# A four-layer graph network on one core: one-hot products of 250 columns in fp32 (728 steps) in place of 500 columns in three bf16 parts (572 steps), and a gathered-row add moved from TensorE to VectorE

## The reference, cut to what matters

```python
h = relu(layernorm(x)); e = edge_attr_16 @ We + be
aggr = segment_sum(relu(h[src] + e), dst)              # layer 0
x = x + gelu((h + aggr) @ W1 + b1) @ W2 + b2
...
wn = w * inv_sqrt_out[src] * inv_sqrt_in[dst]          # layer 1, ten steps
h = 0.9 * segment_sum(h[src] * wn, dst) + 0.1 * h0
...                                                    # layer 2: three attention layers over the edges; layer 3: edge convolution
```

## Time and profile before

| | |
|---|---|
| median of 3 runs | 4460.14 us (4458.2 to 4472.35) |
| span of the profiled execution | 4458.5 us |
| its own time | not listed apart; nothing is known to lie around the span |
| first pass (first to last one-hot and ReLU on VectorE) | about 654 to 1363 us |
| busy over the span | TensorE 71%, VectorE 62%, GpSimd 67%, ScalarE 21% |

### The profile page before, as it was taken

The page is one execution under the profiler, slowest core; times in us unless marked ns, Lnnn a source line. Parts: engine busy times, 40 slices in busy tenths (PEclk is TensorE's granted clock), DMA queues, the critical chain, the costliest instruction groups (busy, mean ns, idle before and its releaser), DMA issues.

```text
span 4458.5 us, 80594 instructions
## 1 busy us (share of the span) xinstructions
PE 3158.4 (71%) x19947; PEld 2109.2 (47%) x19958; DVE 2785.2 (62%) x10030; ACT 933.1 (21%) x3282; POOL 2993.2 (67%) x3059
## 2 busy tenths in 40 slices
PE   1240118888887999999678885888758788566665
PEld 1240004454443444343466664666646666445554
DVE  6970229998894111111688887888878888765554
ACT  0000003443341000000122222222212222112121
POOL 2677767777667888850377774777747777467776
PEclk9999999999997999999899997999979999755555
DMA  4310013333348999999322223222232222211112
GB/s 142 110 45 10 17 63 85 86 87 87 80 88 278 364 355 361 357 358 359 109 63 62 62 62 52 63 62 63 61 51 62 62 62 61 34 32 28 28 28 30
DMA packets 295308, 497.96 MB, mean 112 GB/s; under 512 B 165612, under 2 KB 210541, under 8 KB 293675
## 3 DMA queue, kind: packets, MB, share of 16 engines
q1 hardware_dynamic: 120119, 340.02, 21.7%
q0 software_dynamic: 92160, 115.39, 14.1%
q10 hardware_dynamic: 82800, 40.01, 3.1%
HBM read 435.66 MB, written 59.08 MB: 111 GB/s over the span
## 4 chain that ended last, share of the span: by engine, by line
PE 28%; POOL 25%; issue 19%; DMA 13%; DVE 10%; DVEq 1%; ACT 1%; SPq 1%; POOLq 0%; another core or an unknown queue 0%; ACTq 0%
PE ps L1545 26%; POOL arena L814 18%; DMA arena<-table,arena 10%; POOL rows_dst L797 7%; DMA rows_dst<-stage,arena 1%; DVE arena L1150 1%; DVE arena L1132 1%; PE ps L1730 1%; DMA arena<-in_edge_attr_dram 1%; DVE arena L1149 1%; DVEq L542 1%; DVE arena L1134 1%; DVE arena L1168 1%; DVE arena L1164 1%; DVE arena L1319 0%
## 5 line engine op out<-in xcount | busy, mean ns | idle before, releaser
L814 POOL DMA_INDIRECT arena<-table,arena x2080 | 2091.1, 1005 | 1104.3 <-issue 562.9
L1545 PE MATMUL ps<-arena 128*128 128x96 f32 (+3 forms) x9176 | 1473.3, 337 | 599.7 <-DVE arena L1168 252.4
L1545 PEld LDWEIGHTS ps<-arena 128*128 128x128 f32 (+3 forms) x9176 | 1025.4, 196 | 1017.5 <-issue 641.9
L1545 PE MATMUL ps<-arena,nodes 125*64 125x500 f32 (+2 forms) x3144 | 651.1, 538 | 33.4 <-DMA arena<-dense 22.8
L1150 DVE TENSOR_SCALAR arena<-iota_row_b,arena 128x128 f32<-128x128 bf16 x2080 | 579.9, 297 | 0.0
L768 POOL DMA_INDIRECT rows_src<-stage,stage_at x400 | 477.3, 1193 | 117.1 <-issue 109.3
L797 POOL DMA_INDIRECT rows_dst<-stage,arena x400 | 395.4, 989 | 223.3 <-issue 123.2
L1162 DVE TENSOR_TENSOR arena<-ps,arena 128x256 f32<-128x256 f32 x416 | 176.3, 424 | 531.6 <-DMA arena<-table,arena 516.4
L1149 DVE TENSOR_SCALAR arena<-iota_row_b,arena 128x128 bf16<-128x128 bf16 x1664 | 456.0, 276 | 2.1 <-DVE arena L1302 0.7
L1545 PEld LDWEIGHTS ps<-arena,nodes 125*64 125x64 f32 (+1 forms) x3144 | 242.6, 137 | 353.5 <-issue 321.1
L1251 DVE TENSOR_TENSOR nodes<-nodes,ps 125x256 f32 (+1 forms) x70 | 27.5, 392 | 608.4 <-PE ps L1730 608.4
(11 more groups left out here) (285 smaller groups left out, 3605.4 us busy)
## 6 DMA issues: line engine op xcount, KB each, us to landing
arena<-dense SPq DMA_DIRECT2D x240, 750.0 KB
nodes<-dense SPq DMA_DIRECT2D x60, 750.0 KB
dense<-arena ACTq DMA_DIRECT2D x150, 250.0 KB
arena<-table,arena POOLq DMA_INDIRECT x2080
arena<-dense SPq DMA_DIRECT2D x60, 500.0 KB, 7.7
arena<-rows_dst SPq DMA_DIRECT2D x208, 96.0 KB
arena<-dense SPq DMA_DIRECT2D x6, 2000.0 KB, 21.8
arena<-pair_rows SPq DMA_DIRECT2D x12, 976.6 KB
```

Source lines behind the costliest of these rows:

```text
L814: nc.gpsimd.indirect_dma_start(rows[:, u, k, 0:width], None, frm, bass.IndirectOffsetOnAxis(ap=p[:, c, j, c_other:c_other + 1].bitcast(I32 ...
L1545: return nc.tensor.matmul(to, lhsT, rhs, start=start, stop=stop, skip_group_check=True)
```

## The change

A bin is split for the steps: a step now covers two source blocks (250 columns), so that a destination block has 13 step groups, in place of 7. Eviction still goes by the bins of 4 blocks. A step is one fp32 product (no split of the weight). There are `T - 1 + SBINS - HI` = 715 real steps, padded to 728, 56 per body, 7 in every turn. The tables grow from 576 to 728 entries, and their bank and bin columns are now summed up from per-bin differences (`gone_bank`, `gone_need`). The identity product of the gathered rows goes away; VectorE adds `rows` to the edge term with a tensor_tensor and then makes the ReLU in a second instruction behind a semaphore.

```diff
-PER2 = 11
-PER_U = (5, 6)
+SB, SBG = 2, 13
+SBW = SB * LO
+SBINS = HI * SBG
+SCH = -(-SBINS // LO)
+PER2 = 14
+PER_U = (7, 7)
-TABLE_W = 576
+TABLE_W = STEPS_D
...
-        lhs = carve([128, PER2, 3, 128], BF16)
-        rhs = carve([128, PER2, CW], BF16)
+        lhs = carve([128, PER2, 128])
+        rhs = carve([128, PER2, SBW])
...
-            for g in range(CG):
-                nc.vector.tensor_scalar(rel_key[:, g, :], src_blk, float(-g * CW), None, ALU.add)
-            for part in range(3):
-                link(nc.vector.tensor_copy(w_parts[:, :, part], w_left[:, part, :]))
-                if part < 2:
-                    link(nc.vector.tensor_tensor(w_left[:, part + 1, :], w_left[:, part, :], w_parts[:, :, part], ALU.subtract))
+            for g in range(SBG):
+                ins = nc.vector.tensor_scalar(rel_key[:, g, :], src_blk, float(-g * SBW), None, ALU.add)
+            link(ins)
...
-                    if (first + k) % 2:
-                        nc.vector.scalar_tensor_tensor(
-                            lhs[:, slot], iota_row_b[:].unsqueeze(1).to_broadcast([128, 3, 128]), lo_col[:, bass.ds(tile_at, 1)],
-                            w_parts[:, bass.ds(tile_at, 1), :].rearrange("p o c -> p (o c)").unsqueeze(2).to_broadcast([128, 3, 128]),
-                            ALU.is_equal, ALU.mult)
-                    else:
-                        for part in range(3):
-                            nc.vector.tensor_scalar(lhs[:, slot, part, :], iota_row_b[:], lo_col[:, bass.ds(tile_at, 1)],
-                                                    w_left[:, part, bass.ds(tile_at, 1)], ALU.is_equal, ALU.mult)
-                    nc.vector.tensor_scalar(rhs[:, slot, :], iota_col_h[:], flat_keys[:, bass.ds(key_at, 1)], None,
+                    nc.vector.tensor_scalar(lhs[:, slot, :], iota_row_b[:], lo_col[:, bass.ds(tile_at, 1)],
+                                            w_col[:, bass.ds(tile_at, 1)], ALU.is_equal, ALU.mult)
+                    nc.vector.tensor_scalar(rhs[:, slot, :], iota_col_h[:, 0:SBW], flat_keys[:, bass.ds(key_at, 1)], None,
                                             ALU.is_equal).then_inc(op_ready, 1)
...
                 v.wait_ge(lin_ready, i * U + (u + 1))
-                nc.vector.tensor_scalar(of(msg, u)[:, :, 0:D], lin(u), 0.0, None, ALU.max).then_inc(msg_ready, 1)
+                v.wait_ge(gathered[u], 16 * K * (i + 1))
+                nc.vector.tensor_tensor(of(s1, u)[:, 0], lin(u), rows[:, u, :, 0:D], ALU.add).then_inc(sum_ready, 1)
+                v.wait_ge(sum_ready, i * U + (u + 1))
+                nc.vector.tensor_scalar(of(msg, u)[:, :, 0:D], of(s1, u)[:, 0], 0.0, None, ALU.max).then_inc(msg_ready, 1)
...
-                    for part in range(3):
-                        ins = mm(flat[:, bass.ds(step_at["bank", first + k], CW)], lhs[:, slot, part, :], rhs[:, slot, :], start=False, stop=False)
-                    ins.then_inc(built, 1)
+                    mm(flat[:, bass.ds(step_at["bank", first + k], SBW)], lhs[:, slot, :], rhs[:, slot, :],
+                       start=False, stop=False).then_inc(built, 1)
...
-                mm(ps[:, 4 + u % 2, 0:K * D], of(payT, u), wl0[:].rearrange("p k d -> p (k d)"))
-                pe.wait_ge(gathered[u], 16 * K * (i + 1))
-                mm(lin(u), ident[:], rows[:, u, :, 0:D], start=False).then_inc(lin_ready, 1)
+                mm(ps[:, 4 + u % 2, 0:K * D], of(payT, u), wl0[:].rearrange("p k d -> p (k d)")).then_inc(lin_ready, 1)
```

More of the change, by code:

```diff
@@ L59 @@
 BINS = HI * CG
-PER2 = 11
-PER_U = (5, 6)
+SB, SBG = 2, 13
+SBW = SB * LO
+SBINS = HI * SBG
+SCH = -(-SBINS // LO)
+SBIN_CHUNKS = [(h, min(LO, SBINS - h * LO)) for h in range(SCH)]
+assert SBG == -(-HI // SB) and CB == 2 * SB and CG == -(-SBG // 2)
+PER2 = 14
+PER_U = (7, 7)
 PER_BODY = PER2 * U // 2
 STEPS_D = NB * PER_BODY
-TABLE_W = 576
-assert STEPS_D >= T - 1 + BINS - HI and STEPS_D <= TABLE_W and HI - (CG - 1) * CB == 1
+TABLE_W = STEPS_D
+assert STEPS_D >= T - 1 + SBINS - HI and TABLE_W <= 2 * 512 and HI - (CG - 1) * CB == 1
 EV = 2
@@ L233, in gnn_kernel @@
         iota_t = carve([128, TABLE_W])
[L234 removed]
+        bin_col = carve([128, 5 * SCH])
+        gone = carve([128, 2, SCH])
+        gone_d = carve([128, 2, SCH])
+        gone_g = carve([128, 2, SCH])
+        gone_pair = carve([128, 2, SCH])
+        gone_turn = carve([128, 2, SCH])
+        gone_need = carve([128, SCH])
+        gone_bank = carve([128, SCH])
         start_col = carve([128, 2])
[L236 removed]
+        bin_end_f = carve([1, SBINS])
         tables_from = used[0]
[L239 removed]
+        begun = carve([128, SCH, TABLE_W])
         bin_of = carve([1, TABLE_W])
@@ L1063, in _, with down_by @@
-            for h, n in enumerate((LO, BINS - LO)):
+            def down_by(to, frm, n):
+                link(nc.vector.tensor_scalar(to, frm, 1.0 / n, -(0.5 - 0.5 / n), ALU.mult, ALU.add))
+                link(nc.vector.tensor_scalar(to, to, ROUND, None, ALU.add))
+                link(nc.vector.tensor_scalar(to, to, -ROUND, None, ALU.add))
+            for x in range(2):
+                for h in range(SCH):
+                    ins = nc.vector.tensor_scalar(gone[:, x, h:h + 1], iota_p[:], float(h * LO - x), None, ALU.add)
@@ new lines, in _ @@
+            link(ins)
+            down_by(gone_d, gone, SBG)
+            link(nc.vector.scalar_tensor_tensor(gone_g, gone_d, -float(SBG), gone, ALU.mult, ALU.add))
+            down_by(gone_pair, gone_g, 2)
+            link(nc.vector.scalar_tensor_tensor(gone_g, gone_pair, -2.0, gone_g, ALU.mult, ALU.add))
+            link(nc.vector.scalar_tensor_tensor(gone_d, gone_d, float(CG), gone_pair, ALU.mult, ALU.add))
+            down_by(gone_turn, gone_d, EV)
+            link(nc.vector.scalar_tensor_tensor(gone_turn, gone_turn, -float(EV), gone_d, ALU.mult, ALU.add))
@@ L1064, in _ @@
+            for h, n in SBIN_CHUNKS:
                 ins = nc.vector.tensor_scalar(begun[0:n, h, :], iota_t[0:n, :], bin_col[0:n, h:h + 1], None, ALU.is_ge)
```

81 lines of the change are left out of this document (40 added, 41 removed).

## The result

| | before | after |
|---|---|---|
| median of the runs side by side | 4464.36 us (4 runs, 4458.2 to 4472.35) | 4497.35 us (4 runs, 4495.15 to 4504.7) |
| ratio, 95% interval | | 1.0077 [1.0062, 1.0093] |
| span of the profiled execution | 4458.5 us | 4495.1 us |
| first to last step of the first pass | 657.4 to 1362.3, 704.9 us | 659.8 to 1399.0, 739.2 us |

The changed kernel is 33 us slower; the forecast was 17 to 18 us. The difference is 0.8%, small but clear of its interval. The first and last step are those of the register operation that stands ahead of each dense step in TensorE's queue. I read the pass by them from here on, since they can be counted in every kernel; the forecast's 709 us for the pass before runs from VectorE's first instruction to its last, 4.1 us more.

A forecast was written before the change was run, and what follows sets the result against it. TensorE's queue was to replace VectorE as the first pass's bound: 676 + 33 + 18 = 727 us, 18 over 709. With 1.5 us less before the pass, span 4475 us, forecast 4477 us; range 4422 to 4518 us.

The forecast's parts named there:

- The queue becomes the bound: First pass: TensorE's queue keeps 0.467 us a step, needs 676 us, above VectorE's 648 us.
- rival 1: First pass: VectorE stays the bound as the queue's interval falls to 0.40 us; 36 us less, 4423 us; chance 0.20.
- The gaps of 2.8 and 4.0 us: TensorE's queue between turns: 2.8 us with one group of register loads, 4.0 with two; six long, two short a body.
- The waits on the queue: TensorE in the first pass: 33 us for banks, 3 to fill, 5 for jumps, 10 where VectorE is later.
- The bank term: TensorE's queue waits for the eviction to empty one of two banks: 33 us of the first pass.
- Now it is hidden behind VectorE.: Kernel before, first pass: TensorE's queue needs 557 us, 150 us under the 709 that VectorE sets.
- VectorE's work: VectorE in the first pass: seven steps of 0.51 us, add and longer ReLU 0.37 us more; 5.4 us a turn.
- The refills at the loop's jump: VectorE's queue refilling at a body's start: 5.5 us instead of 3.6, twelve times.
- The prologue, 1.5 us less: Preparation before the first pass: three casts and two linked subtractions go, six keys come; 1.5 us less.
- The clock: TensorE's granted clock in the first pass is kept, 0.96 before; under 0.9 would show the forecast wrong.
- rival 3: TensorE's clock falls: 4686 us at 1.2 GHz throughout, 4503 us for a tenth of the turns; chance 0.08.
- GpSimd: GpSimd's gathers in the first pass take 5.9 us a turn, under TensorE's 6.5: hidden.

The follow-up runs named there:

- a shorter eviction: Changed kernel without the clearing of a bank after its eviction (ScalarE's second copy): 4474.17 us, ratio 1.0046 to the kernel before.
- short queue: No increment behind the bank wait, bank and need in one table, one register load per four steps: changed kernel 4424.7 us, kernel before 4424.9 us.
- the half products: Changed kernel with dense products of 125 columns instead of 250: 4510.19 us (1.0111); also without the increment behind the bank wait: 4470.73 us (1.003).
- the two halves of the change: New steps with the old identity product and one-instruction ReLU: 4508.31 us (1.0118); old steps with the gathered rows added on VectorE: 4500.48 us (1.0093).

## Why the prediction was right in sign and short in size

- **The queue becomes the bound.** Right. The interval (0.467 us forecast, 0.467 to 0.48 in unheld turns) did not fall with the products from three to one, which was what rival 1 needed. With the queue shortened, the change is worth nothing either way (0.9925 and 0.9924), so what it costs shows only beside the long queue. That is not to say that all 34 us are the queue's own time: the waits upon it are among them.
- **The gaps of 2.8 and 4.0 us.** Right where unheld (3.0, 3.8 and 4.0 in the four turns above).
- **The waits on the queue, 33 + 3 + 5 + 10 = 51 us: this term was mis-sized.** The steps take 739.2 us, 743 with the 4.1 us at the ends; less the queue's own 676 that leaves 67. The part that fails is "10 for turns in which VectorE (5.4 to 5.9 us, 11 at a body's start) is the later of the two". TensorE stood idle for VectorE's operand for 44.6 us in 30 pieces, the eviction's part of 20.4 apart. Of the 44.6 us, 27 fall into the first turns of the bodies, some 2 us in each, behind VectorE's 5 to 6 us of idle time at the jump. My own 11 us against a turn of 6.5 would have given more than 10 there. For the other 17 us, a chain is likely but not shown: the queue's loads delay VectorE first (47.0 us in front of L1201), and VectorE then is late for TensorE's steps. Split as above, the forecast has 291 us inside the turns and 385 between, ahead of its waits; measured are 334 and 405. The bank term, 33 us, is neither borne out nor refuted: 20.4 us of idle time carry the eviction's name, and a shorter eviction gave 17 us.
- **"Now it is hidden behind VectorE."** Wrong in part. The short queue made the kernel before 31 us faster in its pass (704.9 to 674.0), and an added increment made it 27 slower. VectorE was its fullest engine, but TensorE's queue of 557 us was felt: 17 us went with the increment, inside the turns, and 14 more with the loads.
- **VectorE's work.** Forecast at 5.4 to 5.6 us a turn. Busy in the window: 470 / 600 x 739.2 / 104 = 5.6. Operands start 0.25 and 0.26 us apart as forecast, the addition takes 423 ns and the ReLU follows 0.44 us behind it. The addition alone, in the old kernel, cost 36 us of the pass, 0.35 us a turn; that this is close to my 0.37 is luck, since some 22 of them lie behind the jumps.
- **The refills at the loop's jump.** Forecast at 5.5 us twelve times. VectorE's "issue" wait before its first copy was 29.9 us in 7 pieces, the longest 5.9. At five more jumps the same copy came after 5.3 to 6.0 us of idle time that the profile puts down to TensorE (L1169, 51.9 us in all, the longest 6.0). So ten jumps show 5.0 to 6.0 us, as forecast, and what it waited for at those five can't be told apart. The step that failed is not the refill but what follows from it for TensorE, above.
- **The prologue, 1.5 us less.** Not decided: the first step came 2.4 us later, but kernels with the same preparation stage began their steps anywhere from 658.2 to 666.5 us.
- **The clock.** Kept only roughly, and this term stays open. The granted clock was 0.92 in the middle of the pass, 0.96 before; the bound that I had set (0.9) was not passed. But the stretches at 1.2 GHz grew from 44 to 139 us, some 13 in 100 of the pass more, which is rival 3's small kind (a tenth of the turns, 26 us, 4503 us). The 44 turns with 0.5 us or more of it last 7.41 us and the other 59 last 6.97, but all first turns of a body are among the 44, so this difference is no price of the clock. Nor do the half products give one: their clock was 0.72 and their time 13 us above the kernel after (15 by the ratios), but at 1.2 GHz a step of theirs takes the array 0.43 us, still under the queue's 0.467, where a whole one takes 0.84. The Trainium skill ("TensorE: Matmul & The Clock Gate", HAM oscillation) has gaps between bursts bring the clock down. The trace agrees in part: 0.96, 0.92 and 0.72 go with 504, 460 and 444 us of TensorE busy in 600, but the two halves of the change don't fall in line (0.95 with 462 us, 0.92 with 483).
- **GpSimd.** Hidden, as forecast: it waits 209.5 us in the pass (L827, by the profile for the rows of the destinations), nearly four times the 56 us of before.

What stays open: what bounds the pass of 667 us with the short queue. VectorE is busy there for some 574 us of it (516 of 600 in the window) and loses 41 us at the jumps, where TensorE in turn waits for its operands (36 of its 46.1 us of such waits lie in the first turns of the bodies). Rival 1's sum for a pass bound by VectorE was 673; that is near, but no run changed VectorE's work there. Open, too, is what the stretches at 1.2 GHz cost in the kernel after.

## What to carry to other kernels

An engine's busy share does not contain its queue. Where each step has a wait on a register, an address and loads of registers, measure the interval between two steps' register operations where nothing holds them, count the loads between the turns, and compare this with the engines' busy times before you trade one wide step for more narrow ones. Loads of registers that stand ahead of the first instruction of a round trip can weigh more than a faster step: in the changed kernel one table in place of two gave 41 us on top of the increment's 31, in the kernel before 14 on top of 17 (the loads were never changed alone). VectorE's idle time behind the loop's jump (5 to 6 us) passes on to TensorE once VectorE has no slack left to cover it. And adding one cheap instruction to a suspected queue, in both kernels, tells what share of added queue time the pass pays: 72 in 100 after the change, 31 before. And before a run that is meant to halve an engine's work is read, look in its trace whether it did.

## What the hardware showed that I had not expected

An increment of a semaphore in TensorE's queue costs about 0.15 us a step (0.467 to 0.63, and 0.467 to 0.32 without), a third of the unheld step. Halving an fp32 product's columns from 250 to 125 brought the starts of two products only from 0.211 to 0.206 us at 2.4 GHz.

GpSimd's gathers got faster although nothing of them changed. Their group in the kernel after, in the first pass (busy us, mean ns), beside the median of 1180 ns in the earlier trace rows:

```profile
L827 POOL DMA_INDIRECT arena<-table,arena x413 | 397.8, 963 | 341.9 <-DMA arena<-rows_dst 209.5 <-issue 108.4 <-DMA arena<-table,arena 24.0
```

963 ns against a minimum of 938 ns: nearly every gather now takes its shortest time. The mean before was 1229 ns. What left VectorE are the bf16 operands of 384 and of 500 columns (L1126 and L1134 of the earlier trace rows), and beside the fp32 ones of 128 and 250 columns that came the gathers are hardly stretched. But the operands are not all of it: with the new steps alone the mean is 1042 ns, and with the old operands and the moved addition it is 1128. The Trainium skill ("GPSIMD Engine Reference", Key points) says that GpSimd shares its SBUF interfaces with VectorE and contends with instructions in a 2-port mode or with two SBUF inputs. That the gathers' time follows what VectorE runs agrees with it; which of the two kinds did it, no run here tells apart.
